# Cross-attention kernel: key tiles outermost in attention times V, the next key projection moved between the two row halves, queues reordered to match

## What is computed

```
q = einsum('bcn,dc->bnd', x1, Wq) + bq
k = einsum('bcn,dc->bdn', x2, Wk) + bk[:, None]
v = einsum('bcn,dc->bdn', x2, Wv) + bv[:, None]
attn = softmax(einsum('bnd,bdm->bnm', q, k), axis=2)
out  = einsum('bcm,bnm->bcn', v, attn) + x1
```

## Time and profile before

| | |
|---|---|
| three runs, median (lowest to highest) | 688.91 us (686.63 to 689.27) |
| the profiled execution, span | 687.4 us |
| PE busy | 96% |
| DVE, ACT, POOL busy | 69%, 41%, 20% |
| granted TensorE clock, mean | 0.995 |

### The profile page before, as it was taken

The page is one execution under the profiler, slowest core; times in us unless marked ns, Lnnn a source line. Parts: engine busy times, 40 slices in busy tenths (PEclk is TensorE's granted clock), DMA queues, the critical chain, the costliest instruction groups (busy, mean ns, idle before and its releaser), DMA issues.

```text
span 687.4 us, 8392 instructions
## 1 busy us (share of the span) xinstructions
PE 656.8 (96%) x2848; PEld 534.1 (78%) x2848; DVE 475.1 (69%) x503; ACT 280.7 (41%) x367; POOL 139.3 (20%) x58
## 2 busy tenths in 40 slices
PE   5999889999999989999899998999989999899997
PEld 3877668887788868888688886888868888788886
DVE  4889558695686765876758866679567695686641
ACT  5564422355235352354423633337232364234220
POOL 0302210063001440032400433005130063101200
PEclk9999989999999999999999999999999999999999
DMA  8400932749328482285624675255941749326351
GB/s 317 187 1 12 265 108 61 193 137 243 102 86 232 116 234 91 84 237 124 197 92 123 197 170 190 75 139 158 229 153 61 174 142 248 107 80 149 73 179 56
DMA packets 94874, 100.04 MB, mean 146 GB/s; under 512 B 8336, under 2 KB 69776, under 8 KB 94864
## 3 DMA queue, kind: packets, MB, share of 16 engines
q1 hardware_dynamic: 94864, 99.91, 51.1%
HBM read 51.64 MB, written 16.78 MB: 100 GB/s over the span
## 4 chain that ended last, share of the span: by engine, by line
PE 81%; DVE 6%; issue 4%; SPq 3%; ACT 3%; DMA 2%; DVEq 0%; ACTq 0%
PE acc_ps L731 39%; PE acc_ps L700 25%; PE s_ps L670 8%; PE s_ps L678 4%; PE s_ps L679 4%; DVE pt_lo L455 4%; SPq L208 3%; DMA stage<-in_ctx_dram 2%; ACT pt_hi L302 2%; ACT xs_hi L302 1%; DVE probs L497 1%; DVE blocks L506 1%; PE s_ps L794 1%; DVE negmax L490 1%; ACT probs L337 0%
## 5 line engine op out<-in xcount | busy, mean ns | idle before, releaser
L731 PE MATMUL acc_ps<-pt_hi,vt_hi 128*128 128x512 f32 x512 | 202.0, 395 | 17.5 <-DVE pt_lo L455 17.5
L731 PE MATMUL acc_ps<-pt_hi,vt_lo 128*128 128x512 f32 x512 | 200.5, 392 | 0.0
L731 PE MATMUL acc_ps<-pt_lo,vt_hi 128*128 128x512 f32 x512 | 200.4, 391 | 0.0
L731 PEld LDWEIGHTS acc_ps<-pt_hi,vt_hi 128*128 128x128 f32 x512 | 96.6, 189 | 44.0 <-DVE pt_lo L455 24.1
L337 ACT ACTIVATE probs<-s_ps,negmax 128x1024 f32<-128x1024 f32 x64 | 71.4, 1116 | 128.4 <-DVE negmax L490 128.4
L271 POOL TENSOR_TENSOR xs_lo<-stage,xs_hi 128x1024 fp32r<-128x1024 f32 x35 | 91.1, 2612 | 156.0 <-ACT xs_hi L302 156.0
L731 PEld LDWEIGHTS acc_ps<-pt_hi,vt_lo 128*128 128x128 f32 x512 | 96.7, 189 | 20.4
L731 PEld LDWEIGHTS acc_ps<-pt_lo,vt_hi 128*128 128x128 f32 x512 | 96.8, 189 | 19.8
L271 POOL TENSOR_TENSOR pt_lo<-pt_raw,pt_hi 128x1024 fp32r<-128x1024 f32 x14 | 41.0, 2946 | 327.5 <-ACT pt_hi L302 327.5
L700 PE MATMUL acc_ps<-wv_hi,xs_hi 128*128 128x512 f32 x256 | 99.9, 390 | 0.0
L700 PE MATMUL acc_ps<-wv_hi,xs_lo 128*128 128x512 f32 x256 | 99.7, 389 | 0.0
(11 more groups left out here) (49 smaller groups left out, 602.4 us busy)
## 6 DMA issues: line engine op xcount, KB each, us to landing
pt_raw<-blocks SPq DMA_DIRECT2D x240, 128.0 KB, 2.4
stage<-in_ctx_dram SPq DMA_DIRECT2D x32, 512.0 KB, 5.3
o_sb<-in_x_dram SPq DMA_DIRECT2D x64, 256.0 KB, 3.3
out_dram<-o_sb SPq DMA_DIRECT2D x64, 256.0 KB, 2.6
stage<-in_x_dram SPq DMA_DIRECT2D x28, 512.0 KB, 5.9
blocks<-in_x_dram SPq DMA_DIRECT2D x4, 512.0 KB, 8.6
pt_raw<-in_L_xattn_Wv_dram SPq DMA_DIRECT2D x4, 256.0 KB, 8.0
pt_raw<-in_L_xattn_Wk_dram SPq DMA_DIRECT2D x1, 128.0 KB, 3.4
```

Of the source, the lines that this page charges most:

```text
L731: mm = nc.tensor.matmul(acc_ps[:, c % BANKS, :], v[:, m, cols], p[:, m, :], start=(m == 0 and v is vt_hi and p is pt_hi), stop=(m == MT - ...
```

## The change

PE's `out_part` calls are reordered: m is now the outer loop and c the inner, so that all four accumulators are open at once and close together (`out_row`). `k_next` moves from inside half 1 (before c = 1) to between the halves. The scores of the next batch go behind rows 2, 3, 4 and 5 of half 1. On ACT, `p_hi(b, 1, 0)` and `p_hi(b, 1, 1)` go ahead of `q_cross`, and the other two behind `round_x2` 3. On DVE, `p_lo` 0 and 1 of half 1 go ahead of `q_sum`, all four `out(b, 0, c)` behind `low_x2`, and all four `out(b, 1, c)` behind `turn(nb, 2)`. SP and POOL keep their order.

```diff
--- before.py
+++ after.py
@@ -377,19 +377,17 @@
                 if not last:
                     round_x1(nb, 2)
                     round_x1(nb, 3)
+                p_hi(b, 1, 0)
+                p_hi(b, 1, 1)
+                if not last:
                     q_cross(nb)
                     round_x2(nb, 0)
                     q_high(nb)
-                p_hi(b, 1, 0)
-                if not last:
                     round_x2(nb, 1)
-                p_hi(b, 1, 1)
-                if not last:
                     round_x2(nb, 2)
+                    round_x2(nb, 3)
                 p_hi(b, 1, 2)
                 p_hi(b, 1, 3)
-                if not last:
-                    round_x2(nb, 3)
                 if last:
                     return
 
@@ -554,42 +552,36 @@
                 if not last:
                     low_x1(nb, 1)
                     low_x1(nb, 3)
-                out(b, 0, 0)
-                out(b, 0, 1)
+                p_lo(b, 1, 0)
+                p_lo(b, 1, 1)
                 if not last:
                     dve.wait_ge(s_klo, nb * 2)
                     q_sum(nb)
                     q_low(nb)
-                out(b, 0, 2)
-                for j in range(PAIRS - 1):
-                    p_lo(b, 1, j)
-                p_lo(b, 1, PAIRS - 1)
+                p_lo(b, 1, 2)
                 if not last:
                     low_x2(nb, KT - 1).then_inc(s_x2lo_last, 1)
-                out(b, 0, 3)
-
-                out(b, 1, 0)
+                for c in range(CT):
+                    out(b, 0, c)
+                p_lo(b, 1, 3)
                 if not last:
                     dve.wait_ge(s_qlo, nb + 1)
                     k_sum(nb)
                     k_low(nb)
-                out(b, 1, 1)
+                    neg_max(nb, 0)
+                    normalise(nb, 0)
+                    neg_max(nb, 1)
+                    turn(nb, 0)
+                    normalise(nb, 1)
+                    neg_max(nb, 2)
+                    turn(nb, 1)
+                    normalise(nb, 2)
+                    neg_max(nb, 3)
+                    turn(nb, 2)
+                for c in range(CT):
+                    out(b, 1, c)
                 if last:
-                    out(b, 1, 2)
-                    out(b, 1, 3)
                     return
-                neg_max(nb, 0)
-                normalise(nb, 0)
-                neg_max(nb, 1)
-                turn(nb, 0)
-                out(b, 1, 2)
-                normalise(nb, 1)
-                neg_max(nb, 2)
-                turn(nb, 1)
-                normalise(nb, 2)
-                neg_max(nb, 3)
-                turn(nb, 2)
-                out(b, 1, 3)
                 normalise(nb, 3)
                 turn(nb, 3)
 
@@ -736,6 +728,10 @@
                 elif c == CT - 1 and m % 2:
                     mm.then_inc(s_used, 1)
 
+            def out_row(b, h, m):
+                for c in range(CT):
+                    out_part(b, h, c, m)
+
             def q_next(b):
                 pe.wait_ge(s_exp, b * ST - 1)
                 for k in range(KT):
@@ -762,26 +758,23 @@
             def batch(b, last):
                 nb = b + 1
 
-                for c in range(CT):
-                    for m in range(MT):
-                        if (c, m) == (2, 0) and not last:
-                            q_next(nb)
-                        out_part(b, 0, c, m)
-
-                for c in range(CT):
-                    for m in range(MT):
-                        if not last:
-                            if (c, m) == (1, 0):
-                                k_next(nb)
-                            if (c, m) == (2, 3):
-                                scores_first(nb, 0)
-                            if (c, m) == (2, 6):
-                                scores_first(nb, 1)
-                            if (c, m) == (3, 1):
-                                scores_next(nb, 2)
-                            if (c, m) == (3, 5):
-                                scores_next(nb, 3)
-                        out_part(b, 1, c, m)
+                for m in range(MT):
+                    if m == 4 and not last:
+                        q_next(nb)
+                    out_row(b, 0, m)
+                if not last:
+                    k_next(nb)
+                for m in range(MT):
+                    out_row(b, 1, m)
+                    if not last:
+                        if m == 2:
+                            scores_first(nb, 0)
+                        elif m == 3:
+                            scores_first(nb, 1)
+                        elif m == 4:
+                            scores_next(nb, 2)
+                        elif m == 5:
+                            scores_next(nb, 3)
                 if last:
                     return
 
```

## The result

The changed kernel takes 741.8 us (median of four runs, 740.5 to 745.7) against 688.7: 1.079 times the time before (95% interval 1.075 to 1.082). The forecast was 741.5. The profiled execution has a span of 743.9 us, 56.5 more than before. It is the longest of the four (745.7); the spans of the others are 738.7 to 740.6, so about 4 of the 56.5 us are this execution's own.

What follows compares the result with a forecast made beforehand. PE, busy 96% of the span, bounds the kernel. Profiled 687.4 us plus first batch 3.0, six batches 30.3, last batch's row 0 2.8, end 2.55 and clock 14 gives 740.0; runs' median 1.5 higher, 741.5, range 710 to 753.

Steps and rivals of the forecast that it cites:

- What is removed: PE's waits for `pt_lo` in half 1 go: 17.5 us by themselves, about 24 with slow matmuls and restarts.
- Cost 2: Before `k_next`, x2's rounding stands behind `p_hi`, which waits for half 1's moves; each batch's half 1 ends 5.05 us later.
- Cost 1: Row 0 of half 0 waits 2.8 us for its fourth bank, freed late by `v_lo(7)`; paid only in the last batch.
- Cost 3: At the kernel's end, the last eviction starts later, waiting for its residual: 2.55 us.
- Cost 4: PE's pauses before the end of `k_next` let the clock fall in each of seven batches: 2.0 us each, 14 in all.
- (a): Rival: everything as forecast, but PE's clock stays up in the pauses; 727.5 us, chance 0.25.
- (b): Rival: shorter x2 chain, DVE and POOL taking no turns, and the clock holds; 711.5 us, chance 0.12.
- (c): Rival: x2 and the banks are ready in time, so the kernel gets faster; 665 us, chance 0.03.
- (d): Rival: x2 in time, but row 0 waits 2.8 us in seven batches and the end costs 2.55; 687, chance 0.03.
- (e): Rival: the key chain from `k_sum` to the scores is late as well, 2 us per batch; 755 us, chance 0.07.
- the first batch: Term of the sum: the first batch's half 1 ends 3.0 us later, before any charge for the clock.

Runs made afterwards that it cites:

- f_pairs: Kernel before, with half 1's channel tiles 0 and 1 alternating over the key tiles and the eviction of (1, 0) behind `k_low`; 667.0 us, 0.969.
- g_all: Changed kernel's matmul order with queues on ACT, DVE and SP arranged for it, `k_next` behind two rows of half 1, and scores later; 667.6 us, 0.971.
- a_act: Changed kernel with the old order on ACT and DVE: `q_cross`, `round_x2` 0, `q_high` ahead of `p_hi`, `q_sum`, `q_low` ahead of `p_lo`; 724.6 us, 1.050.
- i_act_sp: Changed kernel with both edits of a_act and b_sp together; 698.6 us, 1.016.
- b_sp: Changed kernel with SP's list alone reordered: residual (1, 3) ahead of the store of (1, 0), next half 0's moves ahead of its residuals; 729.2 us, 1.057.
- j_between: g_all with `k_next` back between the two halves and nothing else moved; 693.0 us, 1.006.
- e_kpos: Changed kernel with `k_next` behind two rows of half 1, half 0's evictions ahead of the third `p_lo`, half 1's spread, scores later; 725.2 us, 1.054.
- h_warm_sp: b_sp with 18 extra unused matmuls in each `k_next`, 9 behind k = 0 and 9 behind k = 1; 717.2 us, 1.042.
- d_before_act: Kernel before, with only ACT's new order (`p_hi` 0 and 1 of half 1 ahead of `q_cross`) and `p_lo` accordingly on DVE; 719.0 us, 1.043.

## Why the prediction was right, point by point

- **What is removed:** right. The waits for `pt_lo` are gone, and f_pairs and g_all, which remove them and add nothing, win 21 and 20 us; the forecast had "about 24".
- **Cost 2, the x2 chain:** right in mechanism and nearly in size. From M to the end of `low_x2` it is 367.53 - 353.36 = 14.2 us; forecast 14.3. DVE and POOL take turns as assumed: POOL's third low part ends at 366.46 (the last row of the chain below), and `low_x2` 1.07 us after it. M itself was S + 22.4 instead of 21.5. Both parts of it are shown by experiments: the order on ACT (a_act, and i_act_sp against b_sp) and the place of `k_next` (j_between, where nothing else moves, and e_kpos).
- **Cost 1, row 0:** the mechanism was right, the size was not. I forecast 2.8 us; the three waits are 3.5, with the restarts PE is 4.4 us late, and in three of batches 1 to 6 the clock falls here too, which makes it 5.5 to 7.0. The term that failed is the start of the moves, E + 5.75. They started at E + 6.7. DVE's transpose was done at E + 6.1, and SP held them for the other 0.6: in its list they stand behind the residual of tile 2 of the next half, which goes into the buffer of tile (1, 2) and waits until the store of that tile has landed. From the start of the moves to the end of `v_lo(7)` it was 24.9 us, 0.45 more than forecast. The chain that ended last shows it (start us, duration us, engine and work; the last row is the low part of cost 2):

```profile
307.69 4.12 DMA out_dram<-o_sb
311.83 0.35 SPq L187
...
312.32 0.63 SPq L208
...
363.13 3.33 POOL xs_lo L271
```

  I had followed DVE's line and not SP's to its end. In batches 1 to 6 PE's lateness in row 0 hid behind the wait for x2; what came through was the late tile 7, whose transpose ended at S + 8.4 instead of 7.05 and made M 0.9 us late (the moves took 14.0 us instead of 14.4). Row 0 shows in the last batch (+6.7 against +2.8; the clock fell there too) and in a_act, where my 699 counted nothing for it and was 26 us too low; with SP's list mended as well it was 698.6.
- **Cost 3, the end:** right; the last eviction waits for its residual (2.9 us against 2.55).
- **Cost 4, the clock:** right that it falls in every batch, as the windows of each of the eight show; 2.0 to 2.3 us each by h_warm_sp against 2.0. But it does not always fall where I had put it: in `k_next` in five of its seven batches, in row 0 in four of the eight (in one batch in both). Where it falls in `k_next`, a good part of its price lies before K. In the batch shown the last 8 matmuls of `k_next` take 3.25 us (366.51 to 369.76) instead of 1.81, K is S + 38.8 (38.6 on average over batches 1 to 6) and not S + 36.8, and from K to E it is 25.8 us on average, 0.4 over the 25.4 at full clock. The rule of the Trainium skill (TensorE: Matmul & The Clock Gate, HAM oscillation), by which a kernel that waits in every tile pays in every tile, holds in this trace: the clock fell in each of the eight batches, outside the first with no pause over 2.1 us.
- **The rivals:** (a), the clock holds, is refuted by the windows and by h_warm_sp; (b), no turns between DVE and POOL, by the 3.36 us of `low_x2` beside POOL; (c) and (d), x2 in time, by the waits. (e), a late key chain, did not come: the scores start without a wait in the trace.
- That the total hit within 1 us owes something to luck: the median of the four runs is 0.3 us off, but the profiled execution, for which the sum was made, is 743.9 against 740.0. M and row 0 were under-priced by about 1 and 2 us a batch; row 0's error costs nothing as long as the x2 chain ends later, the first batch cost 0.7 less than forecast, and in batches 4 and 6 the clock fell in row 0, where PE waits for x2 afterwards anyway, and not in `k_next`.

## What to carry to other kernels

When a loop order is changed so that accumulators close together, follow every in-order queue past the place where their evictions now bunch: a DMA that waits on the bunch (a residual, a store) holds back everything issued behind it. Put a wait for a late transfer behind, not ahead of, work that another chain needs, and keep matmuls that depend on nothing new in front of a projection whose input is late. If two chains end within a few us of each other, undoing one wins little (17 and 13 us here) and undoing both wins much more (43): test them together before calling either harmless.

## What the runs showed of the hardware

- The clock fell without any pause over 2.1 us: in b_sp pauses of 0.1 to 0.9, 2.1 and 2.1 us with 4 matmuls between them brought it to 0.50 in every one of batches 1 to 6, and it costs 2.0 to 2.3 us each time. A pause of 4.58 us behind busy stretches (d_before_act) does the same. Row 0's three waits, 3 matmuls apart, do not decide it by their length: in batches 2, 3 and 5 of the changed kernel (0.9, 0.7 and 1.9 us in batch 3) the clock held there, in batches 1, 4 and 6 (0.4, 0.7 and 1.9 us in batch 6) it fell. What else decides is not shown.
- Matmuls that do nothing useful can pay for themselves: 126 more of them made b_sp 12 us faster. In the changed kernel, where the pauses vary, 140 more brought nothing (748.2 us against 741.8).
- Changing the PSUM bank every third matmul, with four accumulations open, leaves the pace at 0.227 us per matmul (g_all: 79.9 us for 352).
- The same store of 256 KB, that of tile (1, 2), took 2.0 to 2.1 us to land in every batch before, and 4.0 to 4.4 in all but the first of the changed kernel (5.7 there), where other stores and loads of residuals run beside it.
